# Selective scan: VectorE reads of 1024 columns placed between the next pair's scans, the gate one pair later, half of the last pair's read on GpSimd

## The reference

```python
x = silu(causal_conv(x, conv_w, conv_b))
delta = softplus(einsum(dt, dt_w) + dt_b)
A = -exp(A_log)
def step(h, inp):
    u_t, d_t, B_t, C_t = inp
    h = exp(d_t[..., None] * A) * h + (d_t * u_t)[..., None] * B_t[:, None, :]
    y = einsum('bdn,bn->bd', h, C_t)
    return (h, y)
y = selective_scan(x, delta, A, Bm, Cm, D)      # step over the 128 positions, + u * D
y = y * silu(z)
out = einsum(y, out_w)
# forward and reversed sequence are added; rows and columns are added
```

## Time and profile before

| | us |
|---|---|
| median of 3 runs | 28975.46 |
| lowest and highest | 28960.53, 28981.26 |
| profiled execution | 28998.67 |
| its span | 28996.9 |

### The profile page before, as it was taken

The page is one execution under the profiler, slowest core; times in us unless marked ns, Lnnn a source line. Parts: engine busy times, 40 slices in busy tenths (PEclk is TensorE's granted clock), DMA queues, the critical chain, the costliest instruction groups (busy, mean ns, idle before and its releaser), DMA issues. The chain is left out here.

```text
span 28996.9 us, 295604 instructions
## 1 busy us (share of the span) xinstructions
PE 19339.4 (67%) x63642; PEld 5895.2 (20%) x63642; DVE 26552.2 (92%) x29735; ACT 17085.9 (59%) x23617; POOL 24959.7 (86%) x10756
## 2 busy tenths in 40 slices
PE   6666666666666666666666666666666666662583
PEld 1111111111111111111111111111111111110441
DVE  8999999999999999999999999999999999996211
ACT  5666666666666666666666666666666666662032
POOL 8999999999999999999999999999999999993000
PEclk7777777777777777777777777777777777775596
DMA  5555555555555555555555555555555555558557
GB/s 184 193 196 197 194 194 195 193 193 194 194 193 195 193 196 196 195 195 196 194 194 193 196 198 195 196 195 194 195 197 196 196 194 194 195 196 187 108 121 178
DMA packets 1880801, 5506.97 MB, mean 190 GB/s; under 512 B 329944, under 2 KB 593896, under 8 KB 1865704
## 3 DMA queue, kind: packets, MB, share of 16 engines
q1 hardware_dynamic: 1878648, 5484.50, 55.4%
HBM read 4678.40 MB, written 805.31 MB: 189 GB/s over the span
## 5 line engine op out<-in xcount | busy, mean ns | idle before, releaser
L760 POOL TENSOR_TENSOR drive<-du_rep,b_rep 128x1024 f32<-128x1024 f32 x8192 | 19135.2, 2358 | 1397.4 <-DVE state L696 1148.4
L696 DVE TENSOR_TENSOR_SCAN decay<-decay,drive 128x512 f32<-128x512 f32 x11264 | 13129.8, 1211 | 334.5 <-ACT decay L572 172.4
L572 ACT ACTIVATE decay<-delta_rep,a_neg 128x1016 f32<-128x1016 f32 x8192 | 9044.0, 1108 | 2641.9 <-DVE state L696 1720.8
L709 DVE TENSOR_TENSOR read<-decay,c_rep 128x512 f32<-128x512 f32 x11264 | 7115.6, 671 | 0.0
L769 POOL TENSOR_TENSOR read<-state,c_rep 128x1024 f32<-128x1024 f32 x2560 | 6048.2, 2363 | 1.7 <-DVE state L696 1.7
L696 DVE TENSOR_TENSOR_SCAN state<-decay,drive 128x512 f32<-128x512 f32 x5120 | 5948.6, 1201 | 0.0
L435 PE MATMUL y_bank<-read,sel_f 128*32 128x512 f32 x32768 | 4924.1, 728 | 82.1 <-POOL read L769 57.7
L412 PE MATMUL p_bank<-e_one,sel_f 128*128 128x512 f32 x2048 | 1701.0, 925 | 3290.3 <-ACT e_one L555 1859.1
L399 PE MATMUL p_bank<-u,to_dt 128*128 128x512 f32 x2048 | 2119.6, 1138 | 2251.1 <-ACT zs L617 1408.7
L568 ACT COPY decay<-zeros 128x8 f32<-128x8 f32 x5632 | 932.1, 165 | 3773.9 <-DVE read L709 3761.7
L389 PE MATMUL p_bank<-xt,taps 128*128 128x512 f32 x4096 | 2816.3, 824 | 387.2 <-ACT bc L529 384.0
(11 more groups left out here) (89 smaller groups left out, 14397.2 us busy)
## 6 DMA issues: line engine op xcount, KB each, us to landing
du_rep<-du_spread SPq DMA_DIRECT2D x2048, 512.0 KB, 6.3
delta_rep<-delta_spread SPq DMA_DIRECT2D x2048, 512.0 KB, 8.3
b_rep<-bc_spread SPq DMA_DIRECT2D x2048, 512.0 KB, 8.4
c_rep<-bc_spread SPq DMA_DIRECT2D x2048, 512.0 KB, 7.6
du_spread<-e_log SPq DMA_DIRECT2D x512, 512.0 KB, 2.7
delta_spread<-e_one SPq DMA_DIRECT2D x512, 512.0 KB, 3.6
xt<-in_xs SPq DMA_DIRECT2D x1024, 128.0 KB, 3.5
bc_spread<-bc SPq DMA_DIRECT2D x1024, 64.0 KB, 2.0
```

The source lines that it names most:

```text
L572: nc.scalar.activation(inner(place[:, :]), inner(delta_rep[:, j, :]), ACT.Exp, scale=a_neg[s][:, ROW * j + m:ROW * j + m + 1]).then_inc(s_ ...
L696: nc.vector.tensor_tensor_scan(out[:, px(d)][:, ::step], decay[PLACE[h][q]][:, px(d)][:, ::step], drive[:, q % DRIVE_RING, px(d)][:, ::ste ...
L709: nc.vector.tensor_tensor(read[:, q % READ_RING, px(d)], states[:, px(d)], c_rep[:, m, px(d)], ALU.mult).then_inc(s_read_v, 1)
L760: nc.gpsimd.tensor_tensor(drive[:, q % DRIVE_RING, :], du_rep[h][:, j, :], b_rep[:, m, :], ALU.mult).then_inc(s_drive, 1)
```

## The change

Four things change in the scan stage; the work is the same but for the split of one read.

1. VectorE's read of a pair is one instruction of 1024 columns instead of two of 512. Its semaphore counts one per read instead of two.
2. The read of pair q - 1 stands between the forward and the reverse scan of pair q, where it stood after the scans of its own pair. Pair 15's read still follows its own scans.
3. `GATE` is 4 instead of 3.
4. The reverse half of pair 15 (`SHARED`) is scanned into a new SBUF buffer `state_half`, and GpSimd reads it in an instruction of 512 columns. VectorE reads the forward half only. TensorE's rows and ScalarE's decay that takes pair 15's place wait accordingly.

```diff
+SHARED = PAIRS - 1
+def reads_by_pool(q):
+    return pool_before(q) + (q > SHARED)
-GATE, UD = 3, 5
+GATE, UD = 4, 5
+        state_half = sb("state_half", [P, HALF])
 # TensorE, sum_row
-                pe.wait_ge(s_read_v, 2 * NV * U + 2 * vector_before(ROW * m + ROW))
-                pe.wait_ge(s_read_g, NG * U + pool_before(ROW * m + ROW))
+                pe.wait_ge(s_read_v, NV * U + vector_before(ROW * m + ROW))
+                pe.wait_ge(s_read_g, (NG + 1) * U + reads_by_pool(ROW * m + ROW))
 # ScalarE, make_decay
-                    at_least(act, s_read_v, 2 * NV * (U - back) + 2 * vector_before(n) + 2)
+                    if n == SHARED:
+                        at_least(act, s_state, 2 * PAIRS * (U - back) + 2 * n + 2)
+                    at_least(act, s_read_v, NV * (U - back) + vector_before(n) + 1)
 # VectorE, scan and read_state
-            def scan(U, h, q):
+            def scan(U, h, q, d):
...
+                if q == SHARED and d == REV:
+                    at_least(dve, s_read_g, (NG + 1) * U)
+                    to = state_half[:, :]
...
-                for d in range(2):
-                    dve.wait_ge(s_state, 2 * PAIRS * U + 2 * q + d + 1)
-                    nc.vector.tensor_tensor(read[:, q % READ_RING, px(d)], states[:, px(d)],
-                                            c_rep[:, m, px(d)], ALU.mult).then_inc(s_read_v, 1)
+                part = px(FWD) if q == SHARED else slice(0, WIDE)
+                dve.wait_ge(s_state, 2 * PAIRS * U + 2 * q + (1 if q == SHARED else 2))
+                nc.vector.tensor_tensor(read[:, q % READ_RING, part], decay[PLACE[h][q]][:, part],
+                                        c_rep[:, m, part], ALU.mult).then_inc(s_read_v, 1)
 # VectorE, body
-                        scan(U, h, q)
-                        if q not in BY_POOL:
+                        scan(U, h, q, FWD)
+                        if q > 0 and q - 1 not in BY_POOL:
+                            read_state(U, h, q - 1)
+                        scan(U, h, q, REV)
+                        if q == PAIRS - 1:
                             read_state(U, h, q)
 # GpSimd, read_state and body
+                if q == SHARED:
+                    nc.gpsimd.tensor_tensor(read[:, q % READ_RING, px(REV)], state_half[:, :],
+                                            c_rep[:, m, px(REV)], ALU.mult).then_inc(s_read_g, 1)
+                    return
...
+                        if q == SHARED:
+                            read_state(U, h, q)
```

More of the change, by code:

```diff
@@ L200, in scan_stage @@
         s_state = sem("state_halves")
-        s_read_v = sem("read_halves_by_vector")
+        s_read_v = sem("read_by_vector")
         s_read_g = sem("read_by_gpsimd")
@@ L682, in make_du @@
                                         ALU.mult).then_inc(s_evac, 1)
-            def scan(U, h, q):
-                dve.wait_ge(s_decay, PAIRS * U + q + 1)
-                dve.wait_ge(s_drive, PAIRS * U + q + 1)
+            def scan(U, h, q, d):
+                if d == FWD:
+                    dve.wait_ge(s_decay, PAIRS * U + q + 1)
+                    dve.wait_ge(s_drive, PAIRS * U + q + 1)
                 n = pool_before(q)
                 if q in BY_POOL:
-                    at_least(dve, s_read_g, NG * U + n - STATE_RING + 1)
+                    last = n - STATE_RING
+                    at_least(dve, s_read_g, (NG + 1) * (U + last // NG) + last % NG + 1)
                     out = state[:, (NG * h + n) % STATE_RING, :]
@@ L693, in scan @@
                     out = decay[PLACE[h][q]][:, :]
-                for d in range(2):
-                    step = 1 if d == FWD else -1
-                    nc.vector.tensor_tensor_scan(out[:, px(d)][:, ::step],
-                                                 decay[PLACE[h][q]][:, px(d)][:, ::step],
-                                                 drive[:, q % DRIVE_RING, px(d)][:, ::step], 0.0,
-                                                 ALU.mult, ALU.add).then_inc(s_state, 1)
+                step = 1 if d == FWD else -1
+                to = out[:, px(d)]
+                if q == SHARED and d == REV:
+                    at_least(dve, s_read_g, (NG + 1) * U)
+                    to = state_half[:, :]
+                nc.vector.tensor_tensor_scan(to[:, ::step],
+                                             decay[PLACE[h][q]][:, px(d)][:, ::step],
+                                             drive[:, q % DRIVE_RING, px(d)][:, ::step], 0.0,
+                                             ALU.mult, ALU.add).then_inc(s_state, 1)
             def read_state(U, h, q):
                 m, j = group_of(q)
-                states = decay[PLACE[h][q]]
                 dve.wait_ge(s_c[m], 16 * (U + 1))
                 at_least(dve, s_ysum, ROW * U + m - 1)
-                for d in range(2):
-                    dve.wait_ge(s_state, 2 * PAIRS * U + 2 * q + d + 1)
-                    nc.vector.tensor_tensor(read[:, q % READ_RING, px(d)], states[:, px(d)],
-                                            c_rep[:, m, px(d)], ALU.mult).then_inc(s_read_v, 1)
+                part = px(FWD) if q == SHARED else slice(0, WIDE)
+                dve.wait_ge(s_state, 2 * PAIRS * U + 2 * q + (1 if q == SHARED else 2))
+                nc.vector.tensor_tensor(read[:, q % READ_RING, part], decay[PLACE[h][q]][:, part],
+                                        c_rep[:, m, part], ALU.mult).then_inc(s_read_v, 1)
             def gate(U, h, z_taken, projected):
```

## The result

| | before | after |
|---|---|---|
| median, us (20 runs each, side by side) | 28976.3 | 28936.8 |
| lowest and highest | 28953.5, 28992.8 | 28927.9, 28954.8 |
| span of the profiled execution | 28996.9 | 28933.5 |
| mean granted TensorE clock | 0.759 | 0.734 |

The ratio is 0.9987 (95% interval 0.9981 to 0.9993): 40 us less, where 240 were forecast. The time lies in the predicted range and on the predicted side, but the gain is a sixth of the forecast.

A forecast was written before the change was run, and what follows sets the result against it. VectorE and GpSimd were taken as full, with many units bound by the decay chain; 0.44 x 0.24 + 0.56 x 0.65 = 0.47 us over 512 units is 240 us: 28998.7 - 240 - 23 = 28735 us, 80% range 28450 to 28990.

The forecast's parts named there:

- The wide read: VectorE, ten pairs a unit: 1.13 us instead of 1.18 for two narrow reads, saving 0.5 us a unit.
- The half read: Pair 15's reverse half moves to GpSimd: 0.59 us less a unit on VectorE, 1.2 us more on GpSimd.
- GpSimd at 49.9 us a unit: GpSimd's work with the half read, at most 51.0 us; sets the time only if units fell below 49.9.
- The waits at pairs 0 and 1: VectorE waits for ScalarE's decays, 0.27 and 0.79 us; 0.8 to 1.5 us a unit in all.
- The gate one pair later: VectorE's gate at pair 4: same 0.60 us instruction, TensorE's row 0 and u times D still end in time; covered.
- the chain from the reverse product to the decay of pair 2: TensorE, ScalarE and transfer work: unchanged by a faster VectorE, pair 2 starting at 31.86 us as before.
- rival C: TensorE idles 5.7 us, 1.2 GHz reaches the second convolution in every second unit: 340 us slower, about 29310; chance 0.10.
- the 0.24 us of the units bound by the transfer: Units waiting for the decay chain, 44%, shorten from 51.26 to 51.02 us, not by 1.1.
- the 0.65 us of the others: Units that do not wait, 56%, gain between 0.24 and 1.15 us; 0.65 taken as the middle.
- rival B: No difference: the chain gives back 0.24 us, or the half read costs GpSimd 2.32 us; 28920 to 29030, chance 0.18.
- The turns: VectorE's waits without a named releaser, 91.6 us in the stretch, left as they are: no gain counted.

The follow-up runs named there:

- a_warm: Five matmuls of zero weights put behind u times D in every unit of A; 28326.9 us, ratio 0.9776 to the kernel before.
- A: The changed kernel, with all four changes made to the kernel before; 28936.8 us, ratio 0.9987.
- a_gate3: A with the gate back at pair 3, ahead of the forward product; 28944.2 us, ratio 0.9982 to the kernel before.
- B: The kernel before, without the change; median 28976.3 us beside the changed kernel.
- a_warm2: A with two matmuls of zero weights behind u times D in every unit; 28753.3 us, ratio 0.9921 to the kernel before.
- a_early: A with SyncE issuing the delta_rep loads for j = 2 and 3 ahead of its wait for row sum 2; 28939.4 us, ratio 0.9987.
- a_extra: A with one more VectorE memset of 256 columns in each unit, right behind the gate; 28968.0 us, ratio 0.9998.
- a_narrow: A with each wide read split into two of 512 columns at the same place; 29009.9 us, ratio 1.0004.
- b_warm: Four matmuls of zero weights put behind u times D in every unit of B; 28889.9 us, ratio 0.9972.
- b_wide: B with VectorE's reads made 1024 columns wide in the old order, gate at pair 3, no half read; 29320.2 us, ratio 1.0112.
- a_warm_nohalf: a_warm without the half read, VectorE reading all of pair 15 in one wide instruction; 28537.5 us, ratio 0.9844.

## Why the prediction was wrong

**Right.** The wide read: forecast near 1.20 us by duration and 1.13 by starts, measured 1201 ns and 1.13; worth 0.5 us a unit once it can show. The half read: 1.2 us forecast, 1274 ns measured. GpSimd at 49.9 us a unit was forecast: a_warm, where it is the limit, has units of 49.97. The waits at pairs 0 and 1: 0.27 and 0.79 forecast, 0.47 and 0.79 in the unit shown; 1.40 us a unit over the stretch, in the forecast's 0.8 to 1.5. The gate one pair later cost nothing by itself.

**The step that failed** is in the first part: the chain from the reverse product to the decay of pair 2 "starts from the reverse product ... Nothing in it becomes shorter by a faster VectorE", and the sum then took its times unchanged, "as before". Nothing in it became shorter, but something became longer, which that sentence had not asked. TensorE's idle time rose to 5.62 us (rival C had said 5.7), the 1.2 GHz stretch reached row 1's sum, since the clock's rises stayed 51.2 us apart while the units got shorter, and the take moved from 11.15 to between 11.3 and 11.6. That took the 0.24 us of the units bound by the transfer, and all of the 0.65 us of the others, the larger term of the sum (0.56 x 0.65 x 512 = 186 us). "The middle" of 0.24 and 1.15 for units without a wait was the weakest number: no row had been read for how early the chain is in them, nor why. The last fence of this section shows two of them with a shorter idle time ahead of the projection and a high clock there, and the change lengthened just that idle time.

**Rival C** named the mechanism and mis-sized it at +340 us. It let the second convolution fall to 1.2 GHz in every second unit; that convolution stayed at 1.99 us. The loss grows by tenths of a microsecond as the unit gets shorter, so it stops where the unit is back at 51.2 us. Here it took a gain away and did not make the kernel slower. The result is **rival B's** number, no difference, by C's cause.

**The turns** were put at nothing ("I leave VectorE's unnamed waits as they are"). By the lengths of the units they gave 98 us in the profiled execution, more than the whole gain. So this term was missed in the other direction. Whether A would have been slower without it is not shown: a_gate3, with still shorter turns, is no faster than A. That A came out 40 us ahead of B, and not level or behind, was not forecast by any term of the sum and is luck as far as the prediction goes.

**What would have shown it beforehand:** the length of the chain unit by unit, with the idle time and the clock ahead of the projection beside it. In the kernel before, the units at 3345.78 and 3447.90 have 2.75 us of it and a projection at 2.4 GHz (1.05 us), and the take comes 9.87 and 8.93 us after the product; the next projection in the earlier trace rows stands behind 4.44 us, and the take in the earlier trace rows comes at 11.15:

```profile
3345.78 0.66 DVE L681 TENSOR_TENSOR e_log<-p_bank,u 128x512 f32<-128x512 f32 x1
...
3346.49 1.05 PE L404 MATMUL p_bank<-u,xp_t 128*32 128x512 f32 x4 [2.75 <-DVE e_log L681]
...
3355.65 0.69 ACT L520 ACTIVATE u<-p_bank,cols 128x512 f32<-128x512 f32 x1 [1.11 <-PE p_bank L389]
...
3447.90 0.66 DVE L681 TENSOR_TENSOR e_log<-p_bank,u 128x512 f32<-128x512 f32 x1
...
3456.83 0.69 ACT L520 ACTIVATE u<-p_bank,cols 128x512 f32<-128x512 f32 x1 [0.17 <-PE p_bank L389]
```

The take varied by 2.2 us between units of one kernel with the same work: in the last of these the first convolution takes 2.00 us, in the first 3.46, in the earlier trace rows 3.78. The same trace thus showed that the chain has no fixed length. The idle time alone does not tell it: the two units above have the same 2.75 us, and so has the unit of the product at 3498.56, whose projection runs at 1.2 GHz and whose take comes at 11.02. Behind 4.44 us, though, none of 299 units has its take before 11.02. What stays open is the exact size of the effect for a given idle time (a_warm2 missed), why the rises are 51.2 us apart, and what stops VectorE at the turns.

**The better kernel** is a_warm: 0.9776 of the kernel before, and 2.1% under the changed one.

## What to carry to other kernels

Where a chain that sets the end runs over TensorE, read its length in several units, not in one, together with the idle time ahead of it; if it varies with the same work, ask whether the clock is part of it, and whether a faster neighbour engine will only lengthen the idle time. Look also at how far apart the rises of the clock are, against the length of a round of the work. Try filling the gap with matmuls that add zero before judging edits elsewhere: here the wide reads were worth 50 us with the gap and some 260 without. Where two reads are merged into a wide one, put an independent instruction between the read and its last producer: without it the wide reads here cost 1.1%.

## What the runs showed of the hardware

- Kernels that differ by up to 0.6 us of VectorE's work a unit settle near 51.2 us a unit with the turns included (A, a_early and a_gate3 51.21, a_extra 51.30, a_narrow 51.34), and leave it when TensorE's gap is filled: 50.66 in b_warm's body units, 49.97 in a_warm.
- In A the granted clock's first rise behind the reverse product comes 51.2 us after the last one in 507 of 511 units, though the units themselves last from 50.1 to 53.7 us (the very first 48.0).
- Matmuls that do no useful work made a kernel 2.1% faster, though TensorE was already busy for 69% of the stretch (6918.85 us).
- A read of 1024 columns starts 0.12 us later right behind the scan that writes half of its input (b_wide: 2.37 us against 2.25 for two scans; a_warm_nohalf, pair 15: 1.25 against 1.13 for one).
- VectorE's waits without a named releaser, nearly all at the loop's turns, were 91.6 us in 10,000 in B and 0.3 in A; the cause is open.
